# One TensorE order for a convolutional window attention, regrouped by the tile form of its matmuls

## What is computed

```python
def _forward(x, w_qkv, b_qkv, w_dw, b_dw, temperature, w_mlp, b_mlp, w_proj, b_proj):
    qkv = einsum('bchw,oc->bohw', x, w_qkv) + b_qkv           # 1x1, 64 -> 192 channels
    qkv = depthwise_3x3(qkv, w_dw) + b_dw
    q, k, v = windows(qkv)                                    # (windows, 4 heads, 16, 64 pixels)
    attn = softmax(einsum('nhcx,nhdx->nhcd', q, k) * temperature)
    out = einsum('nhcd,nhdx->nhcx', attn, v)
    gate = gelu(einsum('nhcx,yx->nhcy', v, w_mlp) + b_mlp)
    return einsum('bchw,oc->bohw', unwindow(out * gate), w_proj) + b_proj
result = x + _forward(group_norm(x), ...)
```

## Time and profile before

| | |
|---|---|
| median of three runs | 679.08 us (677.62 to 679.31) |
| span of the profiled execution | 680.0 us |
| TensorE matmul busy | 625.8 us, 92% |
| TensorE weight load busy | 549.1 us, 81% |
| VectorE busy | 511.6 us, 75% |
| ScalarE busy | 482.8 us, 71% |

### The profile page before, as it was taken

One profiled execution on the slowest core, in us unless ns is written; L12 is line 12 of the kernel. 1 busy time (PEld: TensorE's weight loads), 2 busy tenths in 40 slices (PEclk: granted clock), 3 DMA queues, 4 the chain that ended last, 5 costly groups with the idle time before them and its releaser, 6 DMA issues.

```text
span 680.0 us, 32438 instructions
## 1 busy us (share of the span) xinstructions
PE 625.8 (92%) x15044; PEld 549.1 (81%) x15044; DVE 511.6 (75%) x790; ACT 482.8 (71%) x631; POOL 0.3 (0%) x5
## 2 busy tenths in 40 slices
PE   3788799999999999999999999999999999999954
PEld 2687698888989898888989898888989798888843
DVE  4872688887888888786878676786868676876684
ACT  3652678787877778786877778786877778786722
POOL 0000000000000000000000000000000000000000
PEclk9997899999999999999999999999999999999975
DMA  9872115335171714132050504132150504112022
GB/s 363 263 217 72 33 50 166 110 86 208 33 232 49 234 59 149 66 102 93 8 191 5 195 4 142 60 94 106 29 173 4 198 3 152 44 50 80 4 82 44
DMA packets 29240, 72.28 MB, mean 106 GB/s; under 512 B 9801, under 2 KB 16329, under 8 KB 24233
## 3 DMA queue, kind: packets, MB, share of 16 engines
q1 hardware_dynamic: 28674, 68.57, 31.0%
q10 hardware_dynamic: 432, 1.65, 0.7%
HBM read 53.44 MB, written 16.78 MB: 103 GB/s over the span
## 4 chain that ended last, share of the span: by engine, by line
PE 87%; ACT 5%; DVE 3%; issue 2%; DMA 1%; ACTq 0%; DVEq 0%
PE unit_ps L709 28%; PE unit_ps L674 26%; PE rest_ps L796 10%; PE rest_ps L787 6%; PE rest_ps L763 6%; PE rest_ps L747 6%; PE rest_ps L773 4%; ACT z L326 2%; DMA patches<-in_hot 1%; ACT dw L326 1%; PE rest_ps L643 1%; PE rest_ps L674 1%; PE unit_ps L636 0%; DVE scores L511 0%; DVE scores L536 0%
## 5 line engine op out<-in xcount | busy, mean ns | idle before, releaser
L326 ACT ACTIVATE z<-unit_ps 100x768 f32<-100x768 f32 x244 | 184.9, 808 | 60.1 <-PE unit_ps L674 60.1
L674 PE MATMUL unit_ps<-consts,patches 64*100 64x192 f32 x1984 | 195.0, 336 | 8.6 <-ACT z L326 6.6
L709 PE MATMUL unit_ps<-z,dw 103*64 103x64 f32 (+2 forms) x6144 | 194.3, 224 | 3.0 <-issue 1.7
L709 PEld LDWEIGHTS unit_ps<-z,dw 103*64 103x64 f32 (+2 forms) x6144 | 185.5, 139 | 10.7 <-issue 8.6
L674 PEld LDWEIGHTS unit_ps<-consts,patches 64*100 64x100 f32 x1984 | 153.6, 164 | 25.8 <-ACT z L326 11.2
L326 ACT ACTIVATE qkv<-unit_ps 128x1024 f32<-128x1024 f32 x78 | 79.1, 1014 | 31.5 <-PE unit_ps L709 31.4
L511 DVE TENSOR_TENSOR scores<-rest_ps,consts 128x512 f32<-128x512 f32 x64 | 44.1, 689 | 51.6 <-PE rest_ps L747 51.6
L503 DVE TENSOR_TENSOR gate<-rest_ps,gate 128x512 f32<-128x512 f32 x64 | 44.1, 689 | 47.5 <-PE rest_ps L787 44.6
L796 PE MATMUL rest_ps<-gate,consts 128*128 128x256 f32 x256 | 75.1, 417 | 1.1 <-DVE gate L503 1.0
L347 ACT ACTIVATE v_t<-rest_ps 128x512 f32<-128x512 f32 x64 | 38.2, 597 | 40.5 <-PE rest_ps L773 38.9
L341 ACT ACTIVATE scores<-scores 128x512 f32<-128x512 f32 x64 | 40.4, 631 | 33.2 <-DVE scores L518 31.6
(11 more groups left out here) (55 smaller groups left out, 530.5 us busy)
## 6 DMA issues: line engine op xcount, KB each, us to landing
staged<-in_x SPq DMA_DIRECT2D x17, 1024.0 KB, 4.9
out_y<-staged SPq DMA_DIRECT2D x15, 1024.0 KB, 5.4
T<-in_x SPq DMA_DIRECT2D x12, 1152.0 KB, 6.7
seen<-in_x SPq DMA_DIRECT2D x32, 256.0 KB, 2.9
qkv<-in_x SPq DMA_DIRECT2D x6, 1024.0 KB, 13.9
T<-in_x SPq DMA_DIRECT2D x3, 1088.0 KB, 6.7
staged<-in_x SPq DMA_DIRECT2D x2, 512.0 KB, 22.9
out_y<-staged SPq DMA_DIRECT2D x4, 256.0 KB, 3.0
```

The costliest lines, as they stand in the source:

```text
L326: return nc.scalar.activation(to, of, ACT.Copy)
L674: last = nc.tensor.matmul(to[0:NPATCH, t, b * QKV:(b + 1) * QKV], patches[image, b, g], w1[image], start=True, stop=True)
L709: last = nc.tensor.matmul(to[h * HW:(h + 1) * HW, m // 8, m % 8 * NW:(m % 8 + 1) * NW], dw[0:used, c, :], z[0:used, c, :], start=True, sto ...
```

## The change

The order on TensorE is rewritten, and some work takes another form or engine so that it can be:

- in the first and second step all eight mix units stand in one stretch between `score` and `apply_probs`;
- `turn_v` becomes a unit itself: eight transposes of 64 rows (form 2x1) into `unit_ps`, copied by `v_up`. It is done for two steps at once, in the first step for the third and the first, in the second for the fourth and the second. VectorE copies the earlier unit, ScalarE the later one. v has four places to stay (`v_ts`) and not one;
- `project` of the step before has the form 2x1 in the first and second step (two halves of 64 rows that add up in PSUM, `project_half`) and 1x2 in the third and fourth (`project`, 64 columns at a time);
- the gates stand in the first and third step in place of the second and fourth, right ahead of `apply_probs`, and one of the two goes to the bank half that `project` uses (`gate_ps`);
- the eighth mix unit of a step is copied by VectorE;
- VectorE adds the gates' bias in the second and fourth step, one of the two ahead of the softmax in the second step and behind its first part in the fourth; `project` waits for that one (`wait_gated`).

The diff, cut to its core:

```diff
+        fill, turns = fillers(i), turns_in(i)
+            order += [*fill[:1], *fill[1:2], *turns, *fill[2:]]
...
+def turns_in(i):
+    return [("turn", j) for j in (i + 2, i)] if i % BATCHES < 2 else []
 def gates_in(i):
-    return (0, 1) if i == 0 else (i + 1, i + 2) if i % 2 and i + 2 < STEPS else ()
+    return [i + 2, i + 3] if i % 2 == 0 and i + 2 < STEPS else []
...
-        turn_ps, proj_ps = pair_ps[:, 0], pair_ps[:, 1]
+        mix_ps, proj_ps = pair_ps[:, :, 0:BATCH * HW], pair_ps[:, :, BATCH * HW:]
-        gate_ps = score_ps[:, :, BATCH * C:]
+        gate_ps = [proj_ps, score_ps[:, :, BATCH * C:]]
...
+        def v_up(engine, copy, i):
+            unit = ("turn", i)
...
+            wait_full(engine, unit)
+            copy(v_ts[i % BATCHES].rearrange("p (h x) -> p h x", h=2),
+                 work[buffer(unit)][:, :, 0:BATCH * HW]).then_inc(free[buffer(unit)], 1)
...
-                    v_up(i)
+                    v_up(act, copy, i)
                     if more:
-                        for g in range(8 * a + 2, 8 * a + 6):
+                        for g in range(8 * a + 2, 8 * a + 7):
                             evacuate_mix(act, copy, n, g)
...
+                now = gates_in(i - 1) if i else [0, 1]
+                if now and a == 1:
+                    gate_up(now[0])
                 scores_up(i)
-                now = gates_in(i)
+                if now and a != 1:
+                    gate_up(now[0])
+                for unit in turns_in(i)[:1]:
+                    v_up(dve, copy, unit[1])
                 if now:
-                    gate_up(now[0])
-                elif i:
+                    gate_up(now[1])
+                if i:
                     residual(i - 1)
                 divide(i)
                 turn(i)
...
+                if n < CHUNKS and a < 2:
+                    evacuate_mix(dve, copy, n, 8 * a + 7)
...
+            def wait_gated(i):
+                pe.wait_ge(mixed_ready, i + 1)
+                for j in gates_in(i)[:1]:
+                    pe.wait_ge(gate_biased, j + 1)
             def project(i):
-                pe.wait_ge(mixed_ready, i + 1)
+                wait_gated(i)
                 for b in range(2):
-                    last = nc.tensor.matmul(proj_ps[:, b * 4 * HW:(b + 1) * 4 * HW], proj[:, b * P:(b + 1) * P],
...
+                    for t in range(2):
+                        last = nc.tensor.matmul(proj_ps[t * C:(t + 1) * C, b],
+                                                proj[:, b * P + t * C:b * P + (t + 1) * C], gated(i, slice(0, P), b),
...
                 score(i)
...
+                elif a < 2:
+                    if i:
+                        fill(units_now[:1])
+                        project_half(i - 1, 0)
+                        fill(units_now[1:2])
+                    fill(turns[:1])
+                    if i:
+                        project_half(i - 1, 1)
+                    fill(turns[1:])
+                    fill(units_now[2:])
+                elif a == 2:
+                    project(i - 1)
+                    fill(units_now)
+                else:
+                    fill(units_now[:1])
+                    project(i - 1)
+                    fill(units_now[1:])
+                for j in gates_in(i):
+                    gates(j, i)
                 apply_probs(i)
```

More of the change, by code:

```diff
@@ L400, in _ @@
                         evacuate_dw(act, copy, n, 4)
-                if more and a == 3:
-                    evacuate_dw(act, copy, n, 5)
+                        evacuate_dw(act, copy, n, 5)
                 if now:
@@ L407, in _ @@
                     evacuate_dw(act, copy, n, 2)
-                if more and a < 2:
-                    evacuate_mix(act, copy, n, 8 * a + 6)
-                    evacuate_mix(act, copy, n, 8 * a + 7)
         @block.vector
@@ L718, in fill @@
                         depthwise(*unit[1:])
+                    elif unit[0] == "turn":
+                        turn_v(unit[1])
                     elif unit[0] == "mean":
@@ L768, in turn_v @@
             def turn_v(i):
-                if i:
-                    pe.wait_ge(mixed_ready, i)
+                unit = ("turn", i)
+                to = take(unit)
                 for g in range(BATCH):
-                    last = nc.tensor.transpose(pair_ps[:, 0, g * P:(g + 1) * P], windows(i, g)[:, 2], ident)
-                last.then_inc(v_t_done, 1)
+                    for h in range(2):
+                        rows = slice(h * HW, (h + 1) * HW)
+                        last = nc.tensor.transpose(to[:, h, g * HW:(g + 1) * HW], windows(i, g)[rows, 2],
+                                                   ident[rows, rows])
+                last.then_inc(full[buffer(unit)], 1)
             def apply_probs(i):
-                pe.wait_ge(v_t_ready, i + 1)
+                wait_free(pe, ("turn", i))
                 pe.wait_ge(probs_t_ready, i + 1)
@@ L799, in project, with project_half @@
                 last.then_inc(proj_done, 1)
+            def project_half(i, second):
+                if second:
+                    pe.wait_ge(half_done, i // BATCHES * 2 + (i % BATCHES == BATCHES - 1) + 1)
+                else:
+                    wait_gated(i)
+                for b in range(2):
+                    rows = slice((b ^ second) * HW, (b ^ second) * HW + HW)
+                    last = nc.tensor.matmul(proj_ps[:, b], proj[rows, b * P:(b + 1) * P], gated(i, rows, b),
+                                            start=not second, stop=bool(second))
+                last.then_inc(proj_done if second else half_done, 1)
```

87 lines of the change are left out of this document (39 added, 48 removed).

## The result

The changed kernel takes **718.97 us** (median of 4 runs, 717.96 to 720.32) against 678.35 for the kernel before (677.38 to 679.31): a ratio of **1.061** (95% interval 1.0586 to 1.0627). The forecast was 715 us, slower with a chance of 0.79. The profiled execution has a span of 718.5 us, 38.5 more than before.

What follows compares the result with a forecast made beforehand. TensorE's own order was taken as the bound; it would lose work but gain waits. Periods without looks (15.8), with looks (13.4), sixth, first and last added 35.8 to 680.0, less 0.9: 715 us; likeliest 702 to 728, range 679 to 738.

Steps and rivals of the forecast that it cites:

- The price list: TensorE's assumed cost per block: half of `project` 0.43 us, turned unit 0.23, 1x2 `project` 0.87, mix unit 0.65.
- The steps: The four steps of a period, walked with waits: 10.6, 10.0, 9.35 and 9.6 us, with 39.5 as their sum.
- the 0.2 of correction on the sum: Added to a period because the same walk through the old order gave 37.8 us against 38.00 measured; result 39.75.
- The pair pace: Long mix stretch: two buffers, each copied before reuse, make a pair of mix units cost 1.80 us, not 1.30.
- The late instructions: VectorE's late product and gate bias: `project` waits 0.6 us in the third step (1.8 with looks), 1.1 in the fourth.
- the looks' part: Two VectorE looks (1.2 us) ahead of the gate product make periods with looks 41.35 us, 3.35 longer than before.
- Rival 1: TensorE alone sets the period, copies and bias coming in time: 33.5 us a period, about 612 us; chance 0.15.
- Rival 2: No change: VectorE is earlier, third- and fourth-step waits (0.57 and 1.1) vanish; 38.05 us a period, about 681; chance 0.07.
- rival 3: Slower still: new forms of `project` and turned units do not run side by side, 3.3 us a period, 765; chance 0.08.
- The sizes of the sum: Added time by kind of period: nine without looks 15.8 us, four with 13.4, sixth 2.2, first 3.4, last 1.0.
- (d): Theory added during the experiments, not in the prediction: in the densest stretch TensorE waits for its own instructions.
- 33.3 us a period: TensorE's own work in a period after the change, form changes included, against 36.8 before by the same prices.

Runs made afterwards that it cites:

- e4: The changed kernel with each mix-unit copy of the loop's steps carrying only half of the channels, the rest of z keeping old values: 691.47 us.
- e6: The changed kernel with the eighth mix copy on ScalarE and the first two steps' last two mix units behind `apply_probs` again: 701.02 us.
- e2: The changed kernel with each step's looks on VectorE ahead of the eighth mix unit's copy instead of at the step's end: 713.92 us.
- e1: The changed kernel with VectorE adding the first gate's bias ahead of the softmax in the fourth step too: 716.61 us.
- e10: e8 with its depthwise units in half as many matmuls of twice the columns: 672.49 us; the kernel before with the same edit took 664.26 us.
- e9: e1 with its depthwise units in 16 matmuls of 128 columns instead of 32 of 64: 699.67 us.
- e7: e1 with the 24 idle products of 192 columns ahead of the loop replaced by 56 of 80 columns, shifting its instruction count: 728.15 us.
- e8: The changed kernel with earlier bias, eighth mix and second depthwise copies on ScalarE, later third-step `project`, and first-step gates and mix units spread: 689.47 us.

## Why the prediction was right

*The price list held.* A half of `project` costs 0.43 (359.72 to 360.15), a turned unit 0.30 (361.05 to 361.35) and 0.24 elsewhere, the 1x2 `project` 0.91 (380.32 to 381.23); assumed were 0.43, 0.23 and 0.87.

*The steps held.* Walked with the 0.2 of correction on the sum: 10.6, 10.0, 9.35, 9.6; measured 10.62, 10.12, 9.27, 9.78. The period was to be 39.75 and is 39.78 when clean; with looks 41.35, measured 41.50 at best and 41.84 on average. The third mix unit was to start 3.98 into the first step and starts at 4.00 (362.37 from 358.37). The pair pace, which carries most of it, was to be 1.80 and is 1.81, and e4 and e6 show that it is the copies' round trip and not TensorE's work: cheaper copies give 27 us, and breaking up the stretch gives 11 in spite of more changes of form.

*The late instructions held.* `project` waits 0.57 in the third step (0.57 forecast) and 1.75 with looks (1.8). In the six fourth steps where TensorE had not stopped in the unit ahead, it waits 0.91 to 1.24 for the bias (1.1 forecast). e2 shows the looks' part, e1 the bias. Rival 1 fell: its period was 33.5, the shortest measured is 6.3 longer. Rival 2 fell with the waits for the product and the bias, rival 3 with the prices of the new forms.

*The sizes of the sum were a little off, in both directions.* From the traces: the nine periods without looks cost 18.5 us (forecast 15.8), the four with looks 15.2 (13.4), the sixth 3.2 (2.2), the last 2.9 (1.0); but the first cost nothing (forecast 3.4). Before, its second step held a wait of 2.91 for ScalarE's copy of a mix unit; the changed kernel has one of 2.83 in its first step instead, for VectorE's copy of a turned unit. The loop's start came 1.1 earlier. Together that is 38.5 against 35.8: the terms that were too small, 7.4 us, were in part offset by the first period and the earlier start, 4.7 us, neither of which was forecast. So it is in part luck that the total came as close as it did. (By its own prices the work before adds up to 36.7 and not 36.8; nothing hangs on it.)

*What the forecast did not have* is (d), 0.34 us a period in the changed kernel, part of it under the bias wait. It was small here because the kernel waited anyway; it became the largest remaining cost as soon as the waits were taken away. The forecast that TensorE, freed of waits, would run at 33.3 us a period is for that reason, and for the steps' own chains, not shown by any run: the best order tried has 35.83 busy in 37.33.

## What to carry to other kernels

Grouping work by form can cost more than the changes of form that it saves when the grouped units share two buffers: ask what stood between them and gave their copies time, and price the stretch by the round trip through the copying engine. When an engine's work is moved to another, list what stands behind it there, the work of only some periods (the looks) too. A control with the same edit in the kernel before belongs beside every experiment that changes the work itself; without it e10 would have read as a gain.

## What the runs showed of the hardware

TensorE's instructions can be the limit. The instruction queue of the trace, in the changed kernel:

```profile
q8 instruction: 122, 2.00, 1.1%
```

That is 16.4 KB a packet. The changed kernel has 122 of them for 31,402 records of TensorE, e9 98 for 25,258: 24 packets fewer for 6,144 records fewer, so 256 a packet. The packets' own records in the changed kernel say 0.9 to 1.5 us each, and none starts sooner than 3.3 us behind the one ahead. Four blocks of one form, two gates, `apply_probs` and `score` (386.93 to 388.97 above), put 128 matmul records and as many weight loads, one packet, into 2.04 us. The fastest 256 records took 1.86 us in the changed kernel and 2.90 in the kernel before, which has no stop inside a unit in its periods.

The traces also tie each stop to a packet. In the 13 kernels of this case TensorE passes 194 modulo 256 behind a packet 1,494 times, and never sooner than 1.1 us after that packet's transfer has ended. All 143 stops, prologues included, end 1.1 to 1.6 us after it.

The Trainium skill, "Runtime: NRT & Kernel Launch", Instruction fetch mechanics, says that instructions come in blocks of 16 KiB (256) and that crossing a block's edge is mostly hidden. The first agrees with the 256; the second does not hold here: a crossing cost 1.69 us in the row of e7 above, and periods are 0.4 to 0.9 us over the clean one in e1, e7 and e8.

What stays open: why a late packet is late. In e8, ahead of the stop at 348.6, TensorE had crossed an edge at 341.25, and its next packet started at 347.81, 6.6 us later; a smaller packet of another instruction queue ran from 340.90 to 341.41, and no run tells whether that held it up. That the stops are waits for instructions is shown by their count (e1, e7), by the packets that they end behind, and by their going from the late periods with fewer instructions (e9, e10); how the fetch is scheduled is not.
